# Two transformer layers on one core: one program block for both layers, the second layer's first tile prepared during the first layer, and new written orders

## The chip, the cores and the metric

The kernel runs on one core of a Trainium2 chip. The metric is the device time of one execution in microseconds (us). A core has five engines with instruction streams of their own: TensorE (PE in the profile, with its weight loads as PEld), VectorE (DVE), ScalarE (ACT), GpSimd (POOL) and SyncE (SP), which only starts DMA transfers here. They wait for each other through semaphores. Each stream is executed in the order in which it is written: an instruction that waits holds up all that stands behind it on its engine.

## The reference, cut to what matters

All numbers are float32. The input x has 4 sequences (b) of 1024 rows of 128 values.

```python
# layer 0
xn = layernorm(x)
qkv = einsum('bse,ehd->bshd', xn, qkv_w) + qkv_b          # 16 heads of 64
probs = softmax(where(causal, q @ k.T / 8, -big))          # per sequence and head, 1024 x 1024
x = x + (probs @ v) @ out_w + out_b + ffn(xn)
# layer 1
xn = layernorm(x)
h = layernorm(xn) * ln_w + ln_b
q, k, v, beta = split(h @ w_slow)                          # 16 heads of 64
# for each s and head, over the 4 sequences b = 0..3 as steps of a recurrence:
#   W += sigmoid(beta) * (v - W @ k) outer k ;  out = W @ q     (q, k: elu + 1, normed to sum 1)
x = x + xn + out @ w_out + moe(xn)                         # 8 experts of 256, best 2 by gate
```

## The kernel before, in words

**Layer 0** first works out the feed-forward part for the four sequences, then the attention in 32 units: a unit is one sequence and one pair of heads. The function `unit(u)` of each engine writes out that engine's share of a unit, and a loop calls it for u = 0 to 32 (the last call only finishes what unit 31 left). A unit handles the 8 row tiles of 128 queries in 5 steps (`STEP_ROWS`): 7; 6 and 0; 5 and 1; 4 and 2; 3. For each step:

- PE writes the scores of both heads into the PSUM tiles `pair0` and `pair1` (`score`, L747). A score matmul contracts over 64 rows, so it uses a 64-row part of the array (64*128 in the profile).
- DVE adds the causal mask (`cover`, L473) and takes the negated maxima of the rows (`maximum`, L482).
- ACT writes the exponentials to SBUF (`softmax`, L369); DVE inverts the sums (`invert`, L500); POOL scales (`scale`, L309).
- PE transposes the probabilities (`flip`, L764, full array) into one of two PSUM tiles, and ACT or DVE copies them to `slots` (`keep_flip`).
- One unit later PE multiplies them by the values (`weigh_high`, L783, for the key tiles lo to hi; `weigh_first`, L807 and L811, for the first four query tiles). These matmuls write 64 columns of the array (128*64 in the profile), one head in either half.
- The output projection (`join`, L829) goes through the PSUM tile `misc`, as do the projections of the next unit (`project`, L712, and `project_values`, L725); DVE adds it into x1 (`add_part`, L517).

Both heads share `pair0` and `pair1` from step to step, so the scores of a step wait until the exponentials of the step before have left their bank.

**Layer 1** is a block of its own, started when all engines have left the first. It works through 8 tiles of 128 positions, each with all 4 sequences. The function `tile(t)` of each engine is called for t = -1 to 8 and writes one fixed pattern, in which parts of tiles t-1, t and t+1 stand mixed. For one tile: DVE takes the statistics (L1453, L1457), POOL turns them into scale and shift (`deviation`, L1142 to L1149), ACT norms (`norm`, `second_norm`), PE transposes, and projects to q, k, v (`project`, L1731) and to the experts (`hidden` L1746, `expert` L1760). POOL multiplies keys and queries of the sequences (`key_products` L1173, `query_products` L1183), DVE sums them per head (`sum_keys` L1562, `sum_queries` L1570) and solves the recurrence in small steps (`mixing`). The values are weighted per sequence r ("row r") by r+1 terms: on DVE (`row`, L1618) for rows 0 and 1 and the first two terms of row 3, on POOL for row 2 (`row2`, L1200) and the other two terms of row 3 (`row3_high`, L1212; `HIGH = 2`). The terms of rows 1 and 2 are added up on POOL (`sums`, L1225) before PE transposes them (`flip_row`, L1790); those of row 3 are transposed one by one and added in PSUM. Last, PE projects out (`join`, L1807), DVE adds (`finish`, L1630; `gather`, L1553 for the experts) and SP writes the tile out.

The tables `PLACES`, `given_at` and `made_at` say which of five PSUM tiles each result uses and in which order; `Tally` objects turn written orders into semaphore counts.

## Time and profile before

| | |
|---|---|
| time, median of 3 runs | 1790.3 us (1790.0 to 1790.69) |
| profiled execution, its own time | 1789.99 us |
| its span, from the first to the last instruction | 1788.3 us |
| PE busy | 1725.7 us (97%) |
| DVE busy | 1309.1 us (73%) |
| ACT busy | 1012.0 us (57%) |
| POOL busy | 838.2 us (47%) |

The span leaves out what lies around the instructions (1.69 us here). PE counts as busy while a matmul is in its pipeline; two matmuls overlap, so rows of PE last longer than the distance from the start of one to the start of the next.

### The profile page before, as it was taken

What the parts mean: (1) busy time and instruction counts of PE and PEld (TensorE: products, weight loads), DVE (VectorE), ACT (ScalarE), POOL (GpSimd) and SP (SyncE); (2) the same over time, 40 slices, a digit from 0 to 9 for tenths busy, and PEclk for the clock granted to TensorE, in tenths of its full rate; (3) what the DMA queues carried; (4) which work ended last, traced back from release to release, by engine and by line L of the source; (5) the groups of instructions that cost most, each with busy time, mean ns of one, the idle gap of its engine ahead of it and who ended that gap; (6) DMA issues with size and microseconds to landing.
All of it is one profiled execution on the core that took longest, in us unless ns stands there. A gap on an engine that the chain in (4) does not pass through costs nothing. (4 is left out here: it accounts for less than half of the span.)

```text
span 1788.3 us, 29509 instructions
## 1 busy us (share of the span) xinstructions
PE 1725.7 (97%) x10026; PEld 1046.3 (59%) x10026; DVE 1309.1 (73%) x2730; ACT 1012.0 (57%) x2043; POOL 838.2 (47%) x681
## 2 busy tenths in 40 slices
PE   7989999999999999999999999987899999999995
PEld 4545555555555555555555555554567767767765
DVE  5466766666676676667666666743999999999994
ACT  2255656665665666566566656645565566565551
POOL 2133332333333233233333323322798798798785
PEclk9999999999999999999999999998999999999997
DMA  8000000000000000000000000001000000000000
GB/s 168 0 1 2 1 1 1 1 1 1 1 1 1 1 1 1 1 1 1 1 1 1 1 1 1 1 1 48 0 1 7 7 1 7 7 1 7 7 0 13
DMA packets 30022, 13.59 MB, mean 8 GB/s; under 512 B 17050, under 2 KB 29364, under 8 KB 29876
## 3 DMA queue, kind: packets, MB, share of 16 engines
q1 hardware_dynamic: 29876, 11.70, 2.9%
q8 instruction: 84, 1.38, 0.3%
q14 instruction: 62, 0.51, 0.1%
HBM read 9.60 MB, written 2.10 MB: 7 GB/s over the span
## 5 line engine op out<-in xcount | busy, mean ns | idle before, releaser
L309 POOL TENSOR_SCALAR probs<-probs,recip 128x128 f32<-128x128 f32 (+5 forms) x448 | 331.0, 753 | 760.9 <-DVE recip L500 760.9
L369 ACT ACTIVATE probs<-pair,neg_max 128x1024 f32<-128x1024 f32 (+6 forms) x448 | 331.6, 749 | 202.1 <-DVE neg_max L482 193.4
L482 DVE TENSOR_REDUCE neg_max<-pair 128x1 f32<-128x256 f32 (+7 forms) x512 | 374.1, 752 | 28.9 <-PE pair L747 12.0
L342 ACT ACTIVATE slots<-flip 128x512 f32<-128x512 f32 x384 | 217.8, 595 | 171.1 <-PE flip L764 98.4
L764 PEld LDWEIGHTS flip<-ident,probs 128*128 128x128 f32 x2048 | 226.2, 141 | 139.8 <-POOL probs L309 83.7
L747 PE MATMUL pair<-qk_sb 64*128 64x512 f32 (+3 forms) x1536 | 291.5, 505 | 2.9 <-ACT probs L369 2.9
L764 PE MATMUL flip<-ident,probs 128*128 128x128 f32 x2048 | 284.3, 277 | 3.5 <-ACT slots L342 2.2
L473 DVE TENSOR_TENSOR pair<-pair,mask 128x128 f32<-128x128 f32 x512 | 135.2, 293 | 192.4 <-PE pair L747 192.2
L783 PE MATMUL accum<-slots,v_sb 128*64 128x512 f32 (+3 forms) x1024 | 233.9, 537 | 1.2 <-ACT slots L342 1.2
L747 PEld LDWEIGHTS pair<-qk_sb 64*128 64x128 f32 x1536 | 125.1, 186 | 110.1 <-issue 71.9
L1183 POOL TENSOR_TENSOR prod<-ks,qs 128x1024 f32<-128x1024 f32 (+3 forms) x32 | 180.2, 5630 | 5.6 <-DVE qs L1522 5.0
L1731 PE MATMUL pair<-slow_sb,h_T 128*128 128x512 f32 x384 | 179.6, 597 | 0.5 <-DVE qs L1522 0.5
L712 PE MATMUL misc<-xnT,w_qk 128*128 128x512 f32 x256 | 137.3, 618 | 3.2 <-DVE v_sb L491 1.7
L783 PEld LDWEIGHTS accum<-slots,v_sb 128*64 128x64 f32 x1024 | 51.2, 135 | 123.6 <-issue 123.5
L1731 PEld LDWEIGHTS pair<-slow_sb,h_T 128*128 128x128 f32 x384 | 70.0, 192 | 78.6 <-issue 69.5
L1173 POOL TENSOR_TENSOR prod<-ks 128x1024 f32<-128x1024 f32 (+2 forms) x24 | 109.2, 4549 | 0.0
L500 DVE RECIPROCAL recip<-row_sum 128x2 f32<-128x2 f32 x256 | 37.6, 158 | 81.4 <-ACT probs L369 81.4
L456 DVE COPY slots<-flip 128x512 f32<-128x512 f32 x128 | 87.5, 686 | 11.5 <-PE flip L764 7.1
L1570 DVE TENSOR_REDUCE misc<-prod 128x16 f32<-128x1024 f32 (+3 forms) x32 | 90.3, 2822 | 5.3 <-POOL prod L1183 5.2
L1371 ACT ACTIVATE e_buf<-pair 128x1024 f32<-128x1024 f32 x64 | 65.4, 1021 | 50.2 <-PE pair L1731 50.2
L369 ACT ACTIVATION_READ_ACCUMULATOR probs<-pair,neg_max 128x1 f32 x448 | 91.2, 204 | 0.0
L1746 PE MATMUL flip<-nrm_T,w_sb 128*128 128x512 f32 x176 | 87.5, 601 | 2.3 <-DVE x L1553 1.2
(167 smaller groups left out, 2619.0 us busy)
## 6 DMA issues: line engine op xcount, KB each, us to landing
x<-in_L_attn_x SPq DMA_DIRECT2D x4, 512.0 KB, 5.1
out<-x SPq DMA_DIRECT2D x8, 256.0 KB, 2.3
slow_sb<-in_L_attn_w_slow SPq DMA_DIRECT2D x3, 512.0 KB, 7.9
w_qk<-in_L_attn_qkv_w SPq DMA_DIRECT2D x2, 512.0 KB, 7.1
w_sb<-in_L_ffn_W SPq DMA_DIRECT2D x1, 1024.0 KB
w_v<-in_L_attn_qkv_w SPq DMA_DIRECT2D x1, 512.0 KB, 7.4
bv_bc<-in_L_attn_qkv_b SPq DMA_DIRECT2D x1, 512.0 KB, 7.5
outw_sb<-in_L_attn_out_w SPq DMA_DIRECT2D x1, 512.0 KB, 7.0
```

The costliest lines, as they stand in the source:

```text
L309: pool.tensor_scalar(part, part, recip[:, u % 2, row, h:h + 1], 0.0, ALU.mult, ALU.add).then_inc(scaled, 1)
L342: act.activation(slot_rows(step, h, f), flips[bank][:].rearrange("p (k q) -> p k q", q=P), ACT.Copy).then_inc(flip_kept[bank], 1)
L369: act.activation(dst, pair[h][:, lo:hi], ACT.Exp, bias=neg_max[:, u % 2, row, h:h + 1], accum_out=row_sum[:, u % 2, row, h:h + 1]).then_in ...
L473: dve.tensor_tensor(pair[h][:, hi - P:hi], pair[h][:, hi - P:hi], mask[:], ALU.add).then_inc(covered, 1)
L482: dve.tensor_reduce(out=neg_max[:, u % 2, row, h:h + 1], in_=pair[h][:, lo:hi], axis=AX.X, op=ALU.max, negate=True).then_inc(max_ready, 1)
L712: pe.matmul(misc[:], lhsT=w_qk[:, c, P * n:P * (n + 1)], rhs=xnT[:, u // PAIRS, 512 * half:512 * (half + 1)], start=True, stop=True).then_ ...
L747: last = pe.matmul(pair[h][:, a:z], lhsT=q[part, P * r:P * (r + 1)], rhs=k[part, a - lo:z - lo], start=True, stop=True)
L764: last = pe.transpose(flips[bank][:, P * k:P * (k + 1)], src[:, P * k:P * (k + 1)], ident[:])
L783: last = pe.matmul(accum[D * h:D * (h + 1), at:512], lhsT=values_of(u, k, h), rhs=slots[:, base + at:base + 512], start=k == 0, stop=k == ...
L1173: pool.tensor_tensor(prod[s % 2][:, 0:s, :], ks[:, 0:s, :], ks[:, s:s + 1, :].broadcast_to([P, s, HD]), ALU.mult).then_inc(prod_ready, 1)
L1183: pool.tensor_tensor(prod[s % 2][:, s:2 * s + 1, :], ks[:, 0:s + 1, :], qs[:, s % 2:s % 2 + 1, :].broadcast_to([P, s + 1, HD]), ALU.mult). ...
L1731: last = pe.matmul(places[k][:, 512 * half:512 * (half + 1)], lhsT=h_T[:, P * s:P * (s + 1)], rhs=slow_sb[:, c, 512 * half:512 * (half + 1 ...
```

## The change

The changed kernel computes the same. Five things differ.

1. **Units of layer 0**: the order in `unit(u)` of PE, DVE, ACT and POOL is another, and some `keep_flip` and `keep_att` calls have moved between ACT and DVE. On PE the 8 key tiles of `weigh_high` stood in 8 pieces and stand in two.
2. **Layer 0 prepares layer 1**: the statistics of x1 are taken right after the last addition of each sequence (`second_statistics` in units 8, 16, 24 and at the end; `second_deviation` on POOL); the first tile is normed for the sequences 0 to 2 in unit 28 (`first_norms`, six ACT instructions), and transposed and kept in the places of unit 32's projections (`flip_first`, `keep_first`). Constants are made in layer 0 as well.
3. **One block** holds both layers. The expert weights are loaded into buffers of layer 0 (`xn`, `w_qk`) as soon as those are free; `ks` and `vs` use `xnT` and `qk_sb`.
4. **Layer 1** has no `tile(t)` any more: all 8 tiles are written out one after the other, each engine in its own order, with new places. Tiles 4 to 7 of the sequence come first (`at_of`), since their additions in layer 0 end first.
5. **Row 3**: `HIGH` is 1 (DVE makes one term, POOL three) and POOL adds up row 3 too (`sums(t, 3)`), so `flip_row` transposes 1 term and not 4. Only in the last tile does DVE make all four terms of row 3, and PE transposes every term of rows 1 to 3.

```diff
+                if u > PAIRS and u % PAIRS == 1 and u < UNITS:
+                    second_deviation(u // PAIRS - 1)
...
+            def first_norms():
+                n = at_of(0)
+                act.wait_ge(second_rstd, B - 1)
+                for k, dst in enumerate((nrm, hat)):
+                    for s in range(B - 1):
+                        last = act.activation(dst[:, s, :], x1[:, s, n, :], ACT.Identity, bias=shift1[:, k, s, n:n + 1],
+                                              scale=rstd1[:, k, s, n:n + 1])
+                    last.then_inc(first_normed, 1)
...
+            def second_statistics(u, g):
+                b = u // PAIRS
+                dve.wait_ge(misc_kept, misc_at(u, "o", g))
+                for r in range(GB * g, GB * (g + 1)):
+                    last = dve.bn_stats(stats[:, r, :], x1[:, b, r, :])
+                counted[0] += 1
+                last.then_inc(stats_step, 1)
+                dve.wait_ge(stats_step, counted[0])
+                for r in range(GB * g, GB * (g + 1)):
+                    last = dve.bn_aggr(var1[:, b, r, :], stats[:, r, :])
+                last.then_inc(second_var, 1)
...
                 def add_part(u, g):
...
+                if u % PAIRS == PAIRS - 1:
+                    second_statistics(u, g)
...
-                    weigh_high(u - 1, 0, 1)
+                weigh_high(u - 1, 0, 2)
...
-                    weigh_high(u - 1, 1, 2)
...
+                weigh_high(u - 1, 2, 8)
...
-HIGH = 2
-SUMMED = (1, 2)
+HIGH = 1
...
                 def sums(t, r):
...
+                if r == 3:
+                    pool.wait_ge(high_ready, t + 1)
...
                 def flip_row(t, r, j):
...
-                    many = 1 if r in SUMMED else r + 1
+                summed = r and t < ROWS - 1
+                pe.wait_ge(sum_ready[r] if summed else terms_ready[r], t + 1)
+                many = 1 if summed else r + 1
...
-                for t in range(-1, ROWS + 1):
-                    tile(t)
+            project(0, 0, 0)
+            project(0, 0, 1)
+            flip_nrm(0)
+            flip_hat(0)
+            make_small(0)
+            hidden(0, 1, 1)
```

On PE, in a unit of layer 0 (units 2 to 30 are alike), before: from the scores of step 0 (`pair<-qk_sb 128x512 x4`) on. `accum<-slots` is a piece of `weigh_high`, `flip<-ident,probs` are transposes, `misc<-` are projections.

```order
L747 MATMUL pair<-qk_sb 128x512 x4
L783 MATMUL accum<-slots,v_sb 64x512 x2
L764 MATMUL flip<-ident,probs 128x128 x8
L783 MATMUL accum<-slots,v_sb 64x512 x2
L712 MATMUL misc<-xnT,w_qk 128x512
L783 MATMUL accum<-slots,v_sb 64x512 x2
L747 MATMUL pair<-qk_sb 128x384 x2
L747 MATMUL pair<-qk_sb 128x128 x2
L747 MATMUL pair<-qk_sb 128x512 x2
L783 MATMUL accum<-slots,v_sb 64x512 x2
L764 MATMUL flip<-ident,probs_last 128x128 x4
L764 MATMUL flip<-ident,probs 128x128 x4
```

The same place of PE after the change, from the scores of step 0 to the end of `weigh_high`:

```order
L870 MATMUL pair<-qk_sb 128x512 x4
L906 MATMUL accum<-slots,v_sb 64x512 x4
L887 MATMUL flip<-ident,probs 128x128 x8
L835 MATMUL misc<-xnT,w_qk 128x512
L887 MATMUL flip<-ident,probs_last 128x128 x4
L870 MATMUL pair<-qk_sb 128x384 x2
L870 MATMUL pair<-qk_sb 128x128 x2
L870 MATMUL pair<-qk_sb 128x512 x2
L906 MATMUL accum<-slots,v_sb 64x512 x6
L906 MATMUL accum<-slots,v_sb 64x384 x2
L906 MATMUL accum<-slots,v_sb 64x256 x2
L906 MATMUL accum<-slots,v_sb 64x128 x2
```

The pieces of `weigh_high` have moved together, and the transposes and projections that stood between them stand before or behind.

On POOL, in one tile of layer 1, before: `terms<-vs,M 128x3072` is row 2, `terms<-terms` are the sums, `terms<-vs,M 128x2048` is the high part of row 3.

```order
L1225 TENSOR_TENSOR terms<-terms 128x1024
L1200 TENSOR_TENSOR terms<-vs,M 128x3072
L1225 TENSOR_TENSOR terms<-terms 128x1024 x2
L1142 TENSOR_TENSOR rstd_l<-mv_l,eps 128x4
L1143 TENSOR_SCALAR rstd_l<-mv_l 128x4
L1144 TENSOR_SCALAR neg_mean<-mv_l 128x4
L1147 TENSOR_TENSOR rstd_l<-rstd_l,minus_half 128x8
L1149 TENSOR_TENSOR shift<-rstd_l,neg_mean 128x8
L1183 TENSOR_TENSOR prod<-ks,qs 128x1024
L1212 TENSOR_TENSOR terms<-vs,M 128x2048
L1173 TENSOR_TENSOR prod<-ks 128x1024
```

On POOL after the change, in a late tile (`xnT` is `ks`, `qk_sb` is `vs`):

```order
L1479 TENSOR_TENSOR terms<-terms 128x1024
L1456 TENSOR_TENSOR terms<-qk_sb,M 128x3072
L1419 TENSOR_TENSOR x<-nrm,x 128x4x128
L1479 TENSOR_TENSOR terms<-terms 128x1024 x2
L1466 TENSOR_TENSOR terms<-qk_sb,M 128x3072
L1441 TENSOR_TENSOR prod<-xnT,qs 128x1024
L1433 TENSOR_TENSOR prod<-xnT 128x1024
L1479 TENSOR_TENSOR terms<-terms 128x1024 x3
L1441 TENSOR_TENSOR prod<-xnT,qs 128x2048
```

The five small instructions of `deviation` are gone from the tile, the high part of row 3 has three terms (3072) and not two (2048), and three more sums follow it.

On PE, where layer 0 ends and layer 1 begins, before: `misc<-outw_sb` is the last output projection of layer 0.

```order
L829 MATMUL misc<-outw_sb,att_T 128x128 x8
L238 UNCONDITIONAL_BRANCH
L1677 UNCONDITIONAL_BRANCH
L1702 MATMUL accum<-ident,hat 128x128 x4
L1690 MATMUL flip<-ident,nrm 128x128 x4
L1715 MATMUL flip<-wg_sb,nrm_T 128x8
```

The same place after the change:

```order
L952 MATMUL misc<-outw_sb,att_T 128x128 x8
L2540 UNCONDITIONAL_BRANCH
L2592 MATMUL pair<-slow_sb,h_T 128x512 x4
L2554 MATMUL flip<-ident,nrm 128x128
L2564 MATMUL accum<-ident,hat 128x128
L2575 MATMUL flip<-wg_sb,nrm_T 128x8
```

Two projections of the first tile stand first, and only one transpose of either kind (the fourth sequence) is left to do there.

## Rows read from the trace of the kernel before

**Rows 1.** The page, part 1: busy us, share of the span, instructions.

```profile
PE 1725.7 (97%) x10026; PEld 1046.3 (59%) x10026; DVE 1309.1 (73%) x2730; ACT 1012.0 (57%) x2043; POOL 838.2 (47%) x681
```

**Rows 2.** Stretches: length, busy PE, PEld, DVE, ACT, POOL; clock, DMA share, GB/s.

```profile
85.95:1157.70 1071.75, 1065.74 (x6519) 597.20 (x6518) 729.88 (x1605) 644.80 (x1479) 359.54 (x492) 1.00 0.00 1
1205.50:1299.40 93.90, 74.14 (x300) 45.38 (x300) 63.94 (x143) 50.74 (x80) 46.96 (x24) 0.89 0.08 23
1299.40:1754.00 454.60, 450.19 (x2488) 316.35 (x2488) 437.57 (x788) 268.46 (x401) 383.28 (x120) 1.00 0.02 5
1754.00:1788.30 34.30, 18.78 (x124) 17.87 (x124) 9.94 (x11) 4.07 (x7) 15.90 (x5) 0.69 0.03 9
```

**Rows 3.** Timeline of PE over one unit: start, length, what, how many records.

```profile
605.94 1.08 PE L783 MATMUL accum<-slots,v_sb 128*64 128x512 f32 x4
...
607.98 1.08 PE L783 MATMUL accum<-slots,v_sb 128*64 128x512 f32 x4
608.99 1.12 PE L712 MATMUL misc<-xnT,w_qk 128*128 128x512 f32 x2
610.04 1.08 PE L783 MATMUL accum<-slots,v_sb 128*64 128x512 f32 x4
...
629.94 1.02 PE L712 MATMUL misc<-xnT,w_qk 128*128 128x512 f32 x2
630.80 1.04 PE L764 MATMUL flip<-ident,probs 128*128 128x128 f32 x8
631.74 1.16 PE L829 MATMUL misc<-outw_sb,att_T 128*128 128x128 f32 x8
...
666.41 1.16 PE L829 MATMUL misc<-outw_sb,att_T 128*128 128x128 f32 x8
```

**Rows 4.** Timeline of PE in unit 31, which has no projections.

```profile
1160.95 1.08 PE L783 MATMUL accum<-slots,v_sb 128*64 128x512 f32 x4
...
1162.98 1.94 PE L783 MATMUL accum<-slots,v_sb 128*64 128x512 f32 x8
1164.85 2.00 PE L747 MATMUL pair<-qk_sb 64*128 64x384 f32 x12
```

**Rows 5.** Timelines of DVE and ACT behind the scores of step 0.

```profile
606.06 2.36 DVE L482 TENSOR_REDUCE neg_max<-pair 128x1 f32<-128x1024 f32 x2 [0.36 <-PE pair L747]
...
608.45 1.11 ACT L369 ACTIVATE probs<-pair,neg_max 128x1024 f32<-128x1024 f32 x1
```

**Rows 6.** Groups of layer 1: count, busy us, mean ns, idle before.

```profile
L1225 POOL TENSOR_TENSOR terms<-terms 128x1024 f32<-128x1024 f32 x24 | 56.7, 2362 | 50.5 <-DVE terms L1618 49.2
...
L1212 POOL TENSOR_TENSOR terms<-vs,M 128x2048 f32<-128x2048 f32 x8 | 29.0, 3624 | 1.2 <-PE flip L1790 1.2
...
L1618 DVE TENSOR_TENSOR terms<-vs,misc 128x2048 f32<-128x2048 f32 x16 | 36.5, 2283 | 3.2 <-PE flip L1790 3.1
...
L1453 DVE BATCH_NORM_STATS2 stats<-x 128x6 f32<-128x128 f32 x32 | 6.9, 278 | 0.8 <-POOL score L1132 0.8
...
L1338 ACT ACTIVATE hat<-x,shift,rstd_l 128x128 f32<-128x128 f32 x32 | 13.1, 486 | 12.4 <-POOL shift L1149 12.4
```

**Rows 7.** Timeline of POOL: the same sum in two tiles that follow each other.

```profile
1362.98 2.37 POOL L1225 TENSOR_TENSOR terms<-terms 128x1024 f32<-128x1024 f32 x1 [6.75 <-DVE terms L1618]
...
1429.09 2.37 POOL L1225 TENSOR_TENSOR terms<-terms 128x1024 f32<-128x1024 f32 x1 [6.74 <-DVE terms L1618]
```

**Rows 8.** Timeline of PE between the layers.

```profile
1202.40 1.16 PE L829 MATMUL misc<-outw_sb,att_T 128*128 128x128 f32 x8
...
1214.22 1.09 PE L1702 MATMUL accum<-ident,hat 128*128 128x128 f32 x4 [8.72 <-ACT hat L1338]
```

**Rows 9.** Timeline of the end: POOL's last product, PE's last transposes, DVE's last addition.

```profile
1743.32 8.88 POOL L1183 TENSOR_TENSOR prod<-ks,qs 128x4096 f32<-128x4096 f32 x1
...
1770.76 3.65 PE L1790 MATMUL flip<-ident,terms 128*128 128x128 f32 x16 [1.64 <-POOL terms L1212]
...
1784.84 0.69 DVE L1630 TENSOR_TENSOR x<-flip,x 128x512 f32<-128x512 f32 x1 [21.36 <-PE flip L1807]
```

More of the change, by code:

```diff
@@ L98, in banks_of, with __init__ @@
     return [k for k in range(2) if lo < 512 * (k + 1) and hi > 512 * k]
+GROUPS = (1, 0)
+EARLY = (('qk', 0, 1), ('qk', 1, 0))
 class Tally:
-    def __init__(self, order, units=UNITS):
+    def __init__(self, order, last=()):
         self.order, self.at, n = order, {}, 0
-        for body in range(-1, units + 1):
+        for body in range(-1, UNITS + 1):
             for key, ahead in order:
-                if 0 <= body + ahead < units:
+                if 0 <= body + ahead < UNITS or (body + ahead == UNITS and key in last):
                     n += 1
@@ L155, in layer0 @@
             (('qk', 0, 0), 1), (('o', 1), -1), (('o', 0), -1),
-    ])
+    ], last=EARLY)
     weighed_at = Tally([
@@ new lines, in values_of, with join @@
+            def values_of(u, k, h):
+                at = 2 * D * (u % 2) + D * h
+                return v_sb[:, u // 2 % 2, k, at:at + D]
+            def join(u, g):
+                if done(u):
+                    return
+                use = misc_at(u, "o", g)
+                misc_at.meet(u, "o", g)
+                if use > 1:
+                    pe.wait_ge(misc_kept, use - 1)
+                pe.wait_ge(att_kept, accum_at(u, g))
+                for r in range(GB):
+                    at = P * ROW_ORDER[g].index(r)
+                    last = pe.matmul(misc[:, P * r:P * (r + 1)], lhsT=att_T[:, g, at:at + P], rhs=outw_sb[:, u % PAIRS, :],
+                                     start=True, stop=True)
+                last.then_inc(misc_made, 1)
@@ L1721, in project @@
-                def project(t, s, c):
-                    if done(t):
-                        return
-                    k, use = given(t, "project", s, c)
-                    given_at[k].meet(t, "project", s, c)
-                    if use > 1:
-                        pe.wait_ge(place_kept[k], use - 1)
-                    n, each = given(t, "hat")
-                    pe.wait_ge(place_kept[n], each)
-                    for half in range(2):
-                        last = pe.matmul(places[k][:, 512 * half:512 * (half + 1)], lhsT=h_T[:, P * s:P * (s + 1)],
-                                         rhs=slow_sb[:, c, 512 * half:512 * (half + 1)], start=True, stop=True)
-                    last.then_inc(place_made[k], 1)
@@ L1864, in _ @@
-                for t in range(-1, ROWS + 1):
-                    tile(t)
+                for n, each in latest(given, t, [("score",)] + [("row", r, j) for j in range(2)]):
+                    pe.wait_ge(place_kept[n], each)
+                dst = places[k][:, P * r:P * (r + 1)]
+                pe.matmul(dst, lhsT=score_T[:, P * r:P * (r + 1)], rhs=b2_sb[:], start=True, stop=False)
+                for n in range(PAIRS):
+                    last = pe.matmul(dst, lhsT=outs_T[:, r, n, :], rhs=wout_sb[:, n, :], start=False, stop=n == PAIRS - 1)
@@ new lines, in join @@
+                last.then_inc(joined, 1)
+            project(0, 0, 0)
+            project(0, 0, 1)
+            flip_nrm(0)
+            flip_hat(0)
+            make_small(0)
+            hidden(0, 1, 1)
+            project(0, 1, 1)
+            hidden(0, 1, 0)
+            hidden(0, 0, 0)
+            project(0, 1, 0)
+            hidden(0, 0, 1)
+            hidden(0, 2, 0)
+            expert(0, 0)
+            project(0, 2, 1)
+            expert(0, 1)
+            hidden(0, 2, 1)
+            project(0, 2, 0)
```

3898 lines of the change are left out of this document (2508 added, 1390 removed), and 22 rows, old and new, of tables (exps_at, prods_at, sums_at).

## The prediction

> **What bounds the kernel now.** I read the page first: PE is busy 97% of the span, the next engine 73% [rows 1]. Such shares are means over unlike stages, so I read the busy times by stretch. The reader is to see three stages. In the units of layer 0 PE is busy for practically the whole stretch (1065.74 of 1071.75 us) at the full clock, and DVE, ACT and POOL have room (730, 645, 360 us). In the steady tiles of layer 1 three engines are nearly full: PE 450.19, DVE 437.57 and POOL 383.28 of 454.6 us. Before and behind them PE is idle for 19.8 of 93.9 and 15.5 of 34.3 us, with the granted clock down to 0.89 and 0.69 on average [rows 2].
>
> Then the timeline of PE. The output projection of one unit starts at 631.74, that of the next at 666.41: a unit takes 34.67 us [rows 3]. The same sum of two tiles of layer 1 starts at 1362.98 and at 1429.09: a tile takes 66.11 us [rows 7]. Between the last projections of layer 0 (from 1202.40) and the end lie 585.9 us [rows 8].
>
> **The units: fewer changes of the array's shape.** The unit has the same matmuls after the change. What can differ is what stands beside what. Scores use 64 rows of the array, `weigh` 64 columns, all else the whole. Four records of `weigh_high` take 1.01 us from start to start (607.98 to 608.99) [rows 3], eight in one run 1.87 (1162.98 to 1164.85) [rows 4]: 0.86 for four, and 0.15 on top for each run. A projection between two such runs takes 1.05 (608.99 to 610.04), among whole-array matmuls 0.86 (629.94 to 630.80), 0.19 less. Eight transposes between two runs take 1.03 (605.94 to 607.98, less 1.01), among whole-array matmuls 0.94 (630.80 to 631.74) [rows 3]. So a guest between two `weigh` runs costs 0.15 + 0.19 or 0.15 + 0.09 us for two changes of shape: 0.12 to 0.17 each.
>
> In the written orders of PE I count the changes of shape in a unit: 23 before, 13 after (the pieces of `weigh_high` have moved together). Ten fewer give 1.2 to 1.7 us; I take 1.5, in the middle. Units 1 to 30 are full ones, in which PE never waits: 30 x 1.5 = **45 us**. Units 0, 31 and the clearing up, where PE waits for others anyway, I count at nothing.
>
> The Trainium skill, "TensorEngine Tiling (Array Packing)", Key Properties, says that changing the tiling mode drains TensorE, and "TensorE: Matmul & The Clock Gate", Single matmul latency, puts such a drain at about 166 ns warm. By these 10 x 0.166 x 30 = 50 us would be gained and not 45, and the time would be 1700; the rows lie at or below that figure.
>
> This is worth something only if nobody makes PE wait at 33.2 us a unit. I walked the new order once with the durations of the rows. After the scores of step 0 (they end at 605.94) DVE's maxima run to 608.42 and ACT's last exponential to 609.56, so the next scores may start 3.6 us later [rows 3, 5]. In the new order 1.87 + 0.94 + 0.86 + 0.47 + 0.15 = 4.3 us of matmuls stand between: 0.7 us to spare. At the other steps I find 0.2 to 1.2 us; least before `project(u + 1, 1, 1)`, since DVE has to reach `keep_values(u + 1, 1)`, which it meets between two maxima, and before both output projections. A walk misses small things, so I add 0.1 us a unit: **+3 us**.
>
> **What is put into the units.** `second_statistics` puts 4 instructions of 278 ns [rows 6] and 4 smaller ones, about 1.3 us, behind each of two additions on DVE in units 8, 16 and 24. Queued behind them are the last mask and maxima of the unit; ACT's last exponentials wait for these, and the next unit's scores for those. Some 1.5 of the 2.6 us find room; I take 1.1 us of stall, three times: **+3.3 us**. `first_norms` are six ACT instructions of 486 ns [rows 6], 2.9 us ahead of the copy that `weigh_high` needs and of the first exponentials of unit 28; 1.1 us of it is idle time: **+1.8 us**. POOL's `second_deviation` and the constants fall into POOL's idle time, two thirds of the stretch [rows 2]; without that cover they would be 3 us three times.
>
> **Layer 1.** I sum it by DVE, which is nearest to full if PE gets shorter. DVE's work now is 63.94 + 437.57 + 9.94 = 511.5 us [rows 2]. Away go the statistics (6.9 us [rows 6] and the aggregates, some 3) and in seven tiles half of a 2.28 us product of row 3 [rows 6], 8.0 us; the last tile has four terms and not two, +2.3, and the first tile's two copies come to DVE, +0.5. That leaves 496.4 us. In the steady stretch DVE was idle for 17.0 us in 6.88 tiles (454.6 / 66.11), 2.5 a tile [rows 2, 7]: 20 us in eight. DVE's stream starts 7.5 us after the first of the last two output projections (one addition, statistics, POOL's deviation, a norm of one column block; before, the first transpose came 11.8 us after it, at 1214.22 [rows 8], and DVE's stream later still), and I allow 3 us of holes behind it, before there is work from the experts. At the end, after DVE's last product: 32 transposes, 6.5 us if the clock is halved again as for the 16 of 3.65 us [rows 9], a copy, the output projection and the addition, 3.3, and 2.8 from there (1785.53) to the end of the span; 1.8 of it are in the 496.4 already: 10.8 us. Sum: 7.5 + 3 + 496.4 + 20 + 10.8 = 537.7 us, say 538, against 585.9: **-48 us**.
>
> Does it hold for the other two? PE loses 24 transposes a tile, of 0.94 / 8 us [rows 3] at most: 66.1 - 2.8 = 63.3. POOL is busy 55.7 us a tile (383.28 / 6.88) [rows 2, 7]; it gets three sums of 2.36, 7.1, and a third term, half of 3.62, 1.8, and loses `deviation`, some 2.5 [rows 6]: 62.1 us. My DVE sum is 64.5 a tile with its idle time. So all three stay just below it. The sums on POOL are paid from its idle time of 10.4 us a tile; 6.75 of that is one wait for DVE [rows 7]. If that wait stays where it is, the cover is gone and a tile takes up to 62.1 + 10.4 = 72.5.
>
> **Sum.** 1789.99 (the profiled execution's own time: 1788.3 and 1.69 around it) - 45 + 3 + 3.3 + 1.8 - 48 = 1705.1. The median of the runs is 0.3 above this execution: **1705 us**.
>
> **The rivals.**
> - *PE waits in the units* (chance 0.2). The pairs' banks go round scores, maxima, exponentials, scores, and my margins are as small as 0.2 us. For it: DVE and ACT instructions have strict places, so one late copy delays the next scores. Against it: before, PE had no wait at all at 34.67. If the new unit takes 34.1, 0.9 more than I say, this is 30 x 0.9 = 27 us: 1732.
> - *Layer 1 gets stuck between three full engines* (0.2). POOL at 62.1 and PE at 63.3 leave no room, and a sum that waits for DVE's row holds up the products that DVE waits for. With tiles of 67 us, 2.5 above mine, 8 x 2.5 = 20 us: 1725.
> - *The grouping gives nothing* (0.07): the 0.15 us belongs to something else than the shape. Then units keep 34.67 and the time is 1705 + 45 = 1750.
> - *Slower* (0.03). POOL's `sums(t, 3)` wait for the whole of row 3; behind them stand the products of the next tile, for which DVE waits, and DVE makes the row after that late: if each tile went round this ring, with nothing beside it, the gain of 85 us would be used up from 64.5 + 85 / 8 = 75.1 us a tile; at 78 us it is 1705 + 8 x 13.5 = 1813. The wait of 6.75 us that exists speaks for it, the written order, in which other products stand between, against.
>
> **How the numbers follow.** The forecast has 0.5, with 1690 to 1718 as its own range: 1.7 and not 1.5 us a unit is -6, DVE's idle time at 1 us a tile -12, a change of shape at 0.12 us +9. The first two rivals reach to about 1735. 1685 to 1735 leaves out the fourth part of the first rival, the last two rivals (0.10) and a little below: 0.2. A difference of 0.2% (3.6 us) is about what can be told from no change here. All cases but the last lie far under the time before: faster 0.96, same 0.01, slower 0.03.
>
> **What would show it.** The start of one unit's output projection to the next: 33.0 to 33.4 us, with no gaps on PE; about 35 in units 8, 16, 24 and 28. A run of 24 records of `weigh_high` without pause. The second layer's steady tiles 64 to 65 us, DVE at 96% or more, POOL above 95%. Between the layers no PE gap over 3 us, and no halved clock there. I am wrong if PE shows gaps that end with ACT's exponentials (first rival), if POOL's sums wait (second), or if the records around a joined run cost as much as before (third).

## The result, and the profile after

The changed kernel takes **1690.7 us** (median of 4 runs, 1689.2 to 1692.2) against 1790.2 before in the same session: a ratio of 0.9445, 95% interval 0.9428 to 0.9461. The forecast was 1705 us, with 1685 to 1735 as its range.

Part 1 of the page, and the chain of the work that ended last, after:

```profile
PE 1655.9 (98%) x9882; PEld 1041.9 (62%) x9882; DVE 1329.2 (79%) x2765; ACT 999.9 (59%) x2009; POOL 885.8 (52%) x683
...
PE 96%; DVE 2%; ACT 1%; issue 1%; DMA 0%; POOL 0%; DVEq 0%; ACTq 0%
```

PE has lost 69.8 us of busy time and still fills 98% of the span [rows 1]. Only 144 of its records are gone, so most of that time is not work that left but work that takes less.

The stretches that answer to [rows 2]: the units up to the last but one first output projection, and three pieces of the second layer.

```profile
85.36:1143.91 1058.55, 1047.05 (x6689) 630.54 (x6689) 780.13 (x1730) 648.74 (x1488) 381.25 (x521) 1.00 0.01 2
1168.00:1230.00 62.00, 60.39 (x260) 35.76 (x259) 55.84 (x105) 42.95 (x65) 47.70 (x19) 0.97 0.00 1
1230.00:1660.00 430.00, 429.66 (x2287) 294.28 (x2286) 418.93 (x746) 271.58 (x404) 420.73 (x109) 1.00 0.02 5
1660.00:1690.40 30.40, 25.28 (x217) 24.05 (x216) 20.93 (x30) 7.95 (x14) 11.22 (x2) 0.98 0.06 19
```

The third row is the one to look at. In 430 us of steady tiles PE is busy 99.9%, DVE 97.4% and POOL 97.8% of the time; before, it was 99%, 96% and 84%. The two stretches beside it have filled up as well, and their mean granted clock is 0.97 and 0.98, no longer 0.89 and 0.69. The clock still falls to 0.50, the lower of its two levels, once between the layers. The first row below is of the changed kernel, the other two of the kernel before, whose second layer has 0.50 in two far longer stretches:

```profile
1174.00:1177.00 3.00, 3.00 (x6) 1.45 (x6) 2.53 (x10) 1.43 (x6) 2.35 (x1) 0.50 0.00 0
```

```profile
1209.00:1225.00 16.00, 8.63 (x28) 6.23 (x29) 0.80 (x7) 6.51 (x17) 3.76 (x6) 0.50 0.39 118
1752.00:1775.00 23.00, 8.97 (x40) 8.26 (x41) 11.24 (x11) 3.44 (x6) 16.10 (x6) 0.50 0.04 11
```

PE over one unit, the same place as in [rows 3]:

```profile
612.37 1.16 PE L952 MATMUL misc<-outw_sb,att_T 128*128 128x128 f32 x8
...
624.89 2.00 PE L870 MATMUL pair<-qk_sb 64*128 64x384 f32 x12
626.82 4.09 PE L906 MATMUL accum<-slots,v_sb 128*64 128x512 f32 x24
630.84 1.09 PE L887 MATMUL flip<-ident,probs 128*128 128x128 f32 x8
...
645.42 0.82 PE L952 MATMUL misc<-outw_sb,att_T 128*128 128x128 f32 x5
```

The 24 records of `weigh_high` stand in one run. From one output projection to the next it is 33.05 us (34.67 before): 1.61 us a unit. Six key tiles in one run take 4.02 us from start to start.

Where the extra work stands, PE does wait. The scores of unit 9's first step, behind the statistics of the sequence that has just ended, and the first `weigh_high` of unit 28, behind `first_norms`:

```profile
387.90 1.13 PE L870 MATMUL pair<-qk_sb 64*128 64x512 f32 x4 [1.15 <-ACT probs_last L437]
```

```profile
1022.78 1.94 PE L906 MATMUL accum<-slots,v_sb 128*64 128x512 f32 x8 [1.77 <-ACT slots L399]
```

The distances with the statistics are 34.49, 34.50 and 34.50 us, that with the norms 35.23; three others are 33.4, all the rest 33.06 up to unit 30.

Between the layers (before: [rows 8]) and at the end ([rows 9]) on PE:

```profile
1163.40 1.16 PE L952 MATMUL misc<-outw_sb,att_T 128*128 128x128 f32 x8
1165.34 1.16 PE L952 MATMUL misc<-outw_sb,att_T 128*128 128x128 f32 x8 [0.78 <-DVE x L620]
1166.33 3.60 PE L2592 MATMUL pair<-slow_sb,h_T 128*128 128x512 f32 x8
1170.88 0.33 PE L2554 MATMUL flip<-ident,nrm 128*128 128x128 f32 x1 [0.95 <-ACT nrm L1650]
...
1680.22 3.66 PE L2642 MATMUL flip<-ident,terms 128*128 128x128 f32 x32
1684.66 0.46 PE L2655 MATMUL accum<-b_sb,score_T 128*128 128x128 f32 x2 [0.78 <-ACT outs_T L1624]
```

The first work of the second layer starts 2.93 us behind the first of the last two output projections, where it was 11.8, and no gap of PE between the layers reaches 1 us.

**Where the 97.9 us of the span are.** The first of the last two output projections starts 39.0 us earlier (1163.40 against 1202.40); from there to the end it is 527.0 us and not 585.9: 58.9 us less. The additions that end a tile (`finish`) cut these 58.9 in three. Up to the first of them the second layer takes 124.5 us (before 157.6), -33.1; the six tiles behind it 62.6 us each (before 65.3 on average), -15.7; the rest 26.6 us (36.7), -10.1.

### The profile page after: what moved, and what is told of

It is laid out like the page before. It is cut to its first block, busy times and chain, and to the rows that moved or that the text cites. A ratio compares the mean times of both kernels' runs of the same rounds, so it can differ in the third digit from the quotient of the medians.

```text
span 1690.4 us, 29061 instructions
## 1 busy us (share of the span) xinstructions
PE 1655.9 (98%) x9882; PEld 1041.9 (62%) x9882; DVE 1329.2 (79%) x2765; ACT 999.9 (59%) x2009; POOL 885.8 (52%) x683
## 4 chain that ended last, share of the span: by engine, by line
PE 96%; DVE 2%; ACT 1%; issue 1%; DMA 0%; POOL 0%; DVEq 0%; ACTq 0%
PE pair L870 16%; PE flip L887 16%; PE accum L906 11%; PE pair L2592 10%; PE misc L835 7%; PE flip L2617 5%; PE flip L2605 4%; PE misc L952 4%; PE misc L848 3%; PE flip L2657 3%; PE accum L930 3%; PE pair L801 3%; PE accum L2605 2%; PE accum L2617 2%; PE accum L934 2%; PE flip L811 1%
## 5 line engine op out<-in xcount | busy, mean ns | idle before, releaser
L363 POOL TENSOR_SCALAR probs<-probs,recip 128x256 f32<-128x256 f32 (+5 forms) x448 | 331.3, 754 | 707.8 <-DVE recip L589 707.7
L437 ACT ACTIVATE probs<-pair,neg_max 128x768 f32<-128x768 f32 (+5 forms) x448 | 331.9, 749 | 210.3 <-DVE neg_max L571 210.3
L571 DVE TENSOR_REDUCE neg_max<-pair 128x1 f32<-128x768 f32 (+7 forms) x512 | 372.7, 754 | 33.2 <-PE pair L870 10.3
L906 PE MATMUL accum<-slots,v_sb 128*64 128x512 f32 (+3 forms) x1024 | 192.9, 519 | 3.5 <-ACT slots L399 3.5
L1441 POOL TENSOR_TENSOR prod<-xnT,qs 128x1024 f32<-128x1024 f32 (+3 forms) x32 | 180.2, 5634 | 6.5 <-DVE xnT L2134 4.8
L534 DVE COPY slots<-flip 128x512 f32<-128x512 f32 x192 | 131.8, 687 | 24.2 <-PE flip L887 20.4
L1433 POOL TENSOR_TENSOR prod<-xnT 128x1024 f32<-128x1024 f32 (+2 forms) x24 | 109.1, 4548 | 10.4 <-DVE xnT L2134 10.4
L1479 POOL TENSOR_TENSOR terms<-terms 128x1024 f32<-128x1024 f32 x42 | 99.2, 2362 | 5.7 <-DVE terms L2220 3.4
L2617 PEld LDWEIGHTS flip<-w_qk,hid 128*128 128x128 f32 x720 | 86.2, 192 | 17.7 <-issue 13.3
L1633 ACT ACTIVATE hid<-flip,columns 128x512 f32<-128x512 f32 x86 | 58.6, 683 | 52.5 <-PE flip L2605 47.5
```

The costliest lines, as they stand in the source:

```text
L363: pool.tensor_scalar(part, part, recip[:, u % 2, row, h:h + 1], 0.0, ALU.mult, ALU.add).then_inc(scaled, 1)
L437: act.activation(dst, pair[h][:, lo:hi], ACT.Exp, bias=neg_max[:, u % 2, row, h:h + 1], accum_out=row_sum[:, u % 2, row, h:h + 1]).then_in ...
L571: dve.tensor_reduce(out=neg_max[:, u % 2, row, h:h + 1], in_=pair[h][:, lo:hi], axis=AX.X, op=ALU.max, negate=True).then_inc(max_ready, 1)
L906: last = pe.matmul(accum[D * h:D * (h + 1), at:512], lhsT=values_of(u, k, h), rhs=slots[:, base + at:base + 512], start=k == 0, stop=k == ...
L1441: pool.tensor_tensor(prod[s % 2][:, s:2 * s + 1, :], ks[:, 0:s + 1, :], qs[:, s % 2:s % 2 + 1, :].broadcast_to([P, s + 1, HD]), ALU.mult). ...
L2617: last = pe.matmul(places[k][:, P * s:P * (s + 1)], lhsT=hid[:, e % 2, j, P * s:P * (s + 1)], rhs=w2_sb[:, e, j, :], start=j == 0, stop=j ...
```

## The experiments

**1. The grouping taken back, in the changed kernel.** Only PE's order of the unit is touched:

```diff
-                weigh_high(u - 1, 0, 2)
+                weigh_high(u - 1, 0, 1)
                 flip(u - 1, 3, 0, 1, 0)
                 flip(u - 1, 3, 1, 1, 1)
+                weigh_high(u - 1, 1, 2)
                 project(u + 1, 1, 0)
+                weigh_high(u - 1, 2, 3)
                 flip(u - 1, 4, 1, 0, 0)
                 score(u, 1, 1)
                 score(u, 1, 0)
-                weigh_high(u - 1, 2, 8)
+                weigh_high(u - 1, 3, 6)
                 flip(u, 0, 0, 1, 1)
+                weigh_high(u - 1, 6, 7)
                 flip(u, 0, 1, 1, 0)
                 project_values(u + 1, 0)
+                weigh_high(u - 1, 7, 8)
```

> The changed kernel with the two runs of weigh_high cut into six pieces again on TensorE (key tiles 0, 1, 2, 3 to 5, 6, 7), with transposes and projections between them: 20 changes of the array's shape in a unit and not 13. Theory (the changes of shape cost 0.12 to 0.17 us each): 7 x 0.16 = 1.1 us a unit, the distance from unit to unit goes from 33.06 to 34.2 us, and the time from 1690.7 to about 1725 us. Rival (the gain of the units is from the other orders, not from the grouping): 33.1 us a unit, about 1691 us. Above 1730 would mean waits of PE.

Measured: 1725.6 us (ratio to before 0.9637, 0.9623 to 0.9652), 34.9 us above the changed kernel. PE's timeline, the output projection of two units that follow each other:

```profile
595.29 1.16 PE L952 MATMUL misc<-outw_sb,att_T 128*128 128x128 f32 x8
...
601.68 1.08 PE L906 MATMUL accum<-slots,v_sb 128*64 128x512 f32 x4
602.69 1.09 PE L887 MATMUL flip<-ident,probs 128*128 128x128 f32 x8
603.71 1.08 PE L906 MATMUL accum<-slots,v_sb 128*64 128x512 f32 x4
...
629.44 1.16 PE L952 MATMUL misc<-outw_sb,att_T 128*128 128x128 f32 x8
```

34.15 us, 1.10 us more for seven changes of shape more, with no wait: 0.156 us each. The same matmuls in another neighbourhood cost that much. The change as a whole gives 1.61 us for ten: 0.161. Counted in the traces, what differs are the changes between 128*64 (64 columns) and the full array: 13 in a unit before, 10 here, 3 in the changed kernel. All other changes of shape together, those from and to the scores' 64*128, are 10 in each of the three. So 0.16 us is what this one kind costs; the price of the others does not follow from these runs.

**2. The grouping alone, in the kernel before.**

```diff
-                    weigh_high(u - 1, 0, 1)
+                    weigh_high(u - 1, 0, 2)
                     flip(u - 1, 3, 0, 1, 0)
                     flip(u - 1, 3, 1, 1, 1)
-                    weigh_high(u - 1, 1, 2)
                     project(u + 1, 1, 0)
-                    weigh_high(u - 1, 2, 3)
+                    flip(u - 1, 4, 0, 0, 0)
                     score(u, 1, 1)
                     score(u, 1, 0)
-                    weigh_high(u - 1, 3, 4)
-                    flip(u - 1, 4, 0, 0, 0)
+                    weigh_high(u - 1, 2, 8)
                     flip(u, 0, 1, 0, 1)
-                    weigh_high(u - 1, 4, 5)
                     project_values(u + 1, 0)
-                    weigh_high(u - 1, 5, 6)
                     flip(u, 0, 1, 1, 0)
                     flip(u - 1, 4, 1, 0, 1)
-                    weigh_high(u - 1, 6, 7)
                     score(u, 2, 1)
                     score(u, 2, 0)
-                    weigh_high(u - 1, 7, 8)
```

> The kernel before with weigh_high in two runs on TensorE (key tiles 0 and 1; 2 to 7) and nothing else changed: 14 changes of shape in a unit and not 23. Theory (shape alone): 9 x 0.16 = 1.4 us a unit, 33.2 us from unit to unit, -43 us, about 1747 us. Rival (the new orders of VectorE and ScalarE are needed for it): PE waits behind copies and exponentials that stand where they stood; 34 to 35 us a unit, 1770 to 1795 us. If the grouping gives nothing: 1790 us without PE waits.

Measured: 1792.7 us, ratio 1.0012 (1.0003 to 1.0021): nothing is gained. A unit takes 34.64 us. But PE's work did get shorter: in the stretch up to the last but one first output projection (1096.90 us before, 1098.48 here) it is busy 1053.37 us and not 1089.64.

```profile
85.95:1184.43 1098.48, 1053.37 (x6678) 626.76 (x6677) 739.01 (x1645) 658.58 (x1514) 369.61 (x506) 1.00 0.00 1
```

```profile
85.95:1182.85 1096.90, 1089.64 (x6680) 610.25 (x6680) 746.26 (x1645) 660.09 (x1514) 369.66 (x506) 1.00 0.00 1
```

The first row is of this kernel, the second of the kernel before over the same stretch. The 36 us that PE saves have turned into idle time. In one unit PE waits 0.52 and 0.63 us, 1.15 together; without them a unit would take 33.49 us, 1.18 less than before, or 0.13 for each of nine changes. Why it is less than the 0.16 of experiment 1 is not shown. The timeline of PE, then that of ACT, show one of the places:

```profile
477.53 0.66 PE L764 MATMUL flip<-ident,probs 128*128 128x128 f32 x4
...
480.56 1.99 PE L747 MATMUL pair<-qk_sb 64*128 64x256 f32 x12 [0.63 <-ACT probs L369]
```

```profile
478.22 0.60 ACT L342 ACTIVATE slots<-flip 128x512 f32<-128x512 f32 x1 [2.37 <-PE flip L764]
478.72 0.36 ACT L369 ACTIVATE probs<-pair,neg_max 128x128 f32<-128x128 f32 x1
...
479.40 1.01 ACT L369 ACTIVATE probs<-pair,neg_max 128x896 f32<-128x896 f32 x1
```

The transpose `flip(u, 0, 1, 0, 1)` now stands behind the long run, at 477.53. ACT's copy of it stands in ACT's order ahead of three exponentials whose maxima were ready, so ACT idles 2.37 us, the exponentials come late, and the next scores wait 0.63 us for them. The grouping moves guests of the run to later places, and the other engines' orders have to follow.

**3. The new orders of the units alone, in the kernel before.** All `unit(u)` functions of PE, DVE, ACT and POOL, the tables that count them and the choice of PSUM tile for each transpose (`FLIP_BANK`) are those of the change; blocks, statistics, norms and the second layer are as before.

> The kernel before with the changed written orders of the units on all engines (and the tables that count them), and nothing else: two blocks, no early statistics or norms, the second layer as before. Theory (the grouping on PE pays when the other engines' orders let it, and owes nothing to the rest of the change): 33.06 us from unit to unit, 30 x 1.6 = -48 us, less what units 0 and 31 lose, about 1745 us. Rival (the units need something of the common block, or the second layer gives time back): 1755 us or more.

Measured: 1743.7 us, ratio 0.9737 (0.9722 to 0.9751), -46.6 us; 33.05 us a unit, and the first of the last two output projections stands at 1155.77 and not at 1202.40. The gain of the units is there to the full without any other part of the change, 7.6 us more than in the changed kernel, 6.5 of it in the four units in which the changed kernel has the extra work. Experiments 1 to 3 together: the fewer changes of shape are the gain, and the orders written anew with them (those of the other engines, and the rest of PE's own) are its condition. Which of the new orders are needed was not tried apart.

**4. Row 3 alone, in the kernel before.** One term on DVE and three on POOL, and POOL adds up row 3.

```diff
-HIGH = 2
-SUMMED = (1, 2)
+HIGH = 1
+SUMMED = (1, 2, 3)
...
                     pool.wait_ge(terms_ready[r], t + 1)
+                    if r == 3:
+                        pool.wait_ge(high_ready, t + 1)
...
                     key_products(t, 1)
+                    sums(t - 1, 3)
                     query_products(t, 1)
```

> The kernel before with only row 3 changed: one term on VectorE, three on GpSimd, and GpSimd adds the four up, so that PE transposes one. Theory A (the moved load alone makes the gain of the second layer): PE 2.7 us a tile less, GpSimd 55.7 + 8.9 = 64.6 us a tile at most, tiles of about 64.6 us and not 66.1, 1776 to 1780 us. Theory B (the fixed pattern of a tile can't take it; the written order is needed): GpSimd keeps part of its 10.4 us of waits a tile, tiles of 67 to 72 us, 1795 to 1835 us.

Measured: 1834.8 us, ratio 1.0247 (1.0232 to 1.0262): 44 us slower. POOL's timeline, the first sum of two tiles that follow each other, as in [rows 7]:

```profile
1440.41 2.37 POOL L1227 TENSOR_TENSOR terms<-terms 128x1024 f32<-128x1024 f32 x1 [6.76 <-DVE terms L1621]
...
1496.27 8.91 POOL L1183 TENSOR_TENSOR prod<-ks,qs 128x4096 f32<-128x4096 f32 x1
1511.94 2.37 POOL L1227 TENSOR_TENSOR terms<-terms 128x1024 f32<-128x1024 f32 x1 [6.76 <-DVE terms L1621]
```

A tile takes 71.53 us. POOL works through 64.8 of them and then waits 6.76 us for DVE's row 1, the wait of before. DVE's timeline has the other half:

```profile
1438.06 2.28 DVE L1621 TENSOR_TENSOR terms<-vs,misc 128x2048 f32<-128x2048 f32 x1
...
1477.36 2.29 DVE L1573 TENSOR_REDUCE misc<-prod 128x32 f32<-128x2048 f32 x1 [5.59 <-POOL prod L1183]
...
1509.59 2.28 DVE L1621 TENSOR_TENSOR terms<-vs,misc 128x2048 f32<-128x2048 f32 x1
```

POOL's product for query row 1 comes only behind the three new sums; DVE waits 5.59 us for it at 1477.36, is late with row 1 at 1509.59 by that, and POOL's sum of row 1 waits for this row. From POOL's sum to DVE's sum it is 36.9 us (1440.41 to 1477.36), from there to POOL's next sum 34.6: this ring of two halves is the tile. What is put into POOL's half makes it longer, while POOL stands idle in DVE's. The granted clock is 0.50 for some 7 us in each of these tiles, but that is not what makes them long: POOL works without a wait through its half (1440.41 to 1477.33) and the one wait of DVE in its half is 0.33 us, for POOL and not for PE.

**5. Row 3 not summed, in the changed kernel.** `sums(t, 3)` is left out for tiles 0 to 6, and `flip_row` transposes its four terms one by one.

```diff
-            sums(0, 3)
...
-                summed = r and t < ROWS - 1
+                summed = r and t < ROWS - 1 and r != 3
                 pe.wait_ge(sum_ready[r] if summed else terms_ready[r], t + 1)
+                if r == 3 and t < ROWS - 1:
+                    pe.wait_ge(high_ready, t + 1)
```

> The changed kernel without the sums of row 3 on GpSimd: PE transposes all four terms of row 3 in tiles 0 to 6, 24 transposes more a tile; GpSimd has 3 sums of 2.36 us less a tile. If PE is the bound of the second layer (what the trace after suggests): 24 x 0.114 = 2.7 us a tile, 19 us in seven, about 1710 us. If VectorE is (my sum before the result): about 1691 us. If GpSimd is: up to 7 x 7 = 50 us less, down to 1645 us.

Measured: 1707.8 us, ratio 0.9539 (0.9523 to 0.9555): +17.1 us for 168 transposes. A steady stretch of it:

```profile
1228.01:1658.01 430.00, 429.66 (x2338) 299.03 (x2337) 405.21 (x727) 268.08 (x397) 362.04 (x86) 1.00 0.02 5
```

PE is full; POOL, with 84%, and DVE, with 94%, have room that buys nothing. So in the written order the move of row 3's sums to POOL is worth 17 us; in the fixed pattern the sums and the third term on POOL together cost 44 (experiment 4).

**6. and 7. A little more work for DVE, and for POOL, in the changed kernel.** Each tile makes one sum over 128x1024 twice (DVE), or adds 128x256 constants twice (POOL); the extra results go to a spare buffer.

```diff
+                if r == 0:
+                    if t:
+                        dve.wait_ge(spare_step, t)
+                    dve.tensor_reduce(out=spare_out[:, 0:H], in_=prod[0][:, 0, :].rearrange("p (h d) -> p h d", h=H),
+                                      axis=AX.X, op=ALU.add).then_inc(spare_step, 1)
```

```diff
+                pool.wait_ge(late_loaded, 16 * 6)
+                for k in range(2):
+                    if t or k:
+                        pool.wait_ge(spare_step, 2 * t + k)
+                    pool.tensor_tensor(spare_out[:].rearrange("p (s e) -> p s e", s=2), wout_sb[:, 0:2, :], wout_sb[:, 2:4, :],
+                                       ALU.add).then_inc(spare_step, 1)
```

> The changed kernel with one more sum over 128x1024 on VectorE in each tile of the second layer (the sum for query row 0 made a second time into a spare buffer), some 1.1 us. If VectorE sets the tiles (my sum): 8 x 1.1 = +9 us, 1700 us. If PE does, with VectorE's 11 us of idle time in 430 as room: +0 to +3 us, 1691 to 1694 us.

> The changed kernel with two more additions of 128x256 on GpSimd in each tile of the second layer (into a spare buffer), some 1.3 us a tile, ahead of the residual. If GpSimd sets the tiles: 8 x 1.3 = +10 us, 1701 us. If PE does and GpSimd has room: +0 to +3 us, 1691 to 1694 us.

The groups of the added instructions (busy us, mean ns), DVE's kernel and POOL's kernel:

```profile
L2178 DVE TENSOR_REDUCE spare_out<-prod 128x16 f32<-128x1024 f32 x8 | 9.7, 1208 | 0.0
```

```profile
L1424 POOL TENSOR_TENSOR spare_out<-wout_sb 128x256 f32<-128x256 f32 x16 | 11.8, 740 | 0.6
```

Measured: 1700.2 us with 9.7 us more on DVE (+9.5), and 1695.4 with 11.8 more on POOL (+4.7). By the medians DVE's time is paid in full, though PE's row of the changed kernel seemed to say that PE alone was the bound. The medians overstate both a little, since the executions of one kernel differ in their mean granted clock, and their times with it. Compared between executions with the same mean clock (0.997), DVE's kernel takes 1700.2 us against 1692.2, +8.0, and POOL's 1695.5, +3.3. PE shows it: in the steady stretch of DVE's kernel its busy time is 424.69 of 430 us, with waits such as

```profile
1261.26 0.66 PE L2648 MATMUL accum<-ident,terms 128*128 128x128 f32 x4 [0.98 <-DVE x L2162]
```

My expectation that DVE's 11 us of idle time would take the work was wrong: in the same stretch of DVE's kernel DVE still idles 11.1 of 430 us. My reading is that this idle time lies in other places than the added work; no run has tried that. Of POOL's addition some 60% to 70% found room. Which of two nearly full engines sets the pace can't be told from the busy times of the page; here both do.

**8. Two blocks again, in the changed kernel.** All engines meet between the layers, and the expert weights are loaded after that.

```diff
             layer1(block, sem, sbuf, kept, early, shared, ended, W1, W2, b2_sb, b2, late, out)
...
+        with nc.Block() as block:
```

> The changed kernel with the second layer in a block of its own again (all engines meet between the layers, and the expert weights start to load only then); first tile, orders and row 3 as changed. Theory (the common block is worth something at the boundary): the last additions, the meeting and the loads of 2 MB stand ahead of the first expert matmuls; +5 to +12 us, 1696 to 1703 us. Rival (the early preparation does it all, and the block is nothing): within 2 us of 1690.7.

Measured: 1697.0 us, ratio 0.9478 (0.9465 to 0.9491), +6.3 us. PE between the layers:

```profile
1165.05 1.16 PE L953 MATMUL misc<-outw_sb,att_T 128*128 128x128 f32 x8 [0.79 <-DVE x L621]
1168.95 5.37 PE L2593 MATMUL pair<-slow_sb,h_T 128*128 128x512 f32 x8 [2.74 <-PEq L78]
```

The first projection starts 5.84 us behind the first of the last two output projections and not 2.93, with a wait of 2.74 us for the meeting. The next eight matmuls then take 5.37 us where they took 3.60: the granted clock is 0.50 from 1170.1 to 1173.4, and again from 1177 to 1183, and its mean in the 62 us from there on is 0.92 (0.97 in the changed kernel). So what the second block costs is the meeting and, behind it, a longer time at the lower clock. I had also expected the loads to stand in the way, but PE's waits up to 1250 us hold none for the expert weights. Between the two profiled executions the part behind the output projection is 5.6 us longer, 532.6 us and not 527.0.

**9. No early first tile, in the changed kernel.** `first_norms` and `flip_first` are left out (`EARLY = ()`); tile 0 is normed, transposed and kept for all four sequences after the last addition. The start of the second layer is written in another order for it: ACT's norms ahead of its first exponentials, PE's transposes ahead of its first projections.

> The changed kernel without the early norms and transposes of the first tile: all four sequences of tile 0 are normed, transposed and kept after the last addition of the first layer (statistics of sequences 0 to 2 still early). Theory (the early tile is worth several us at the boundary): 2.2 us come back in unit 28; behind the last addition stand eight norms of 0.49 us and not two, eight transposes and not two, and full copies ahead of the first projection: +5 to +9 us there, 1694 to 1698 us. Rival (hidden by what else starts there, all the gain of the boundary is the block and the order): 1688 to 1691 us.

Measured: 1696.9 us, ratio 0.9472 (0.9456 to 0.9488), +6.2 us. PE between the layers:

```profile
1162.10 1.16 PE L950 MATMUL misc<-outw_sb,att_T 128*128 128x128 f32 x8
...
1170.11 1.09 PE L2562 MATMUL accum<-ident,hat 128*128 128x128 f32 x4 [4.91 <-ACT hat L1658]
1171.56 1.11 PE L2552 MATMUL flip<-ident,nrm 128*128 128x128 f32 x4 [0.36 <-ACT nrm L1648]
1172.46 5.50 PE L2587 MATMUL pair<-slow_sb,h_T 128*128 128x512 f32 x8
```

The first projection stands 10.4 us behind the first of the last output projections and not 2.9. In this execution 1.6 us more are lost in unit 31, to a lower clock (below), and 1.8 are won in unit 28. From the first of the last output projections to the end it takes 533.4 us, 6.4 more than in the changed kernel, with the granted clock at 0.50 for twice as long. Less the 1.8 of unit 28, the early tile is worth some 4.6 us in this execution, and 6.2 by the medians.

**10. The extra work moved, in the changed kernel.** The statistics go into units 9, 17 and 25, cut in four pieces where DVE idles 0.9 to 1.1 us; `second_deviation` a unit later; `first_norms` behind ACT's first exponentials of unit 28, where ACT otherwise idles 3.3 us.

```diff
-                if u == UNITS - 4:
-                    first_norms()
...
                 keep_flip(u - 1, 3, 1, 1, 1)
+                if u == UNITS - 4:
+                    first_norms()
...
-                if u % PAIRS == PAIRS - 1:
-                    second_statistics(u, g)
...
                 maximum(u, 6, 1)
+                late = u > PAIRS and u % PAIRS == 1 and u < UNITS
+                if late:
+                    take_stats(u // PAIRS - 1, 1)
                 keep_att(u - 1, 1)
                 invert(u, 0)
+                if late:
+                    take_var(u // PAIRS - 1, 1)
...
                 keep_flip(u, 1, 0, 0, 0)
+                if late:
+                    take_stats(u // PAIRS - 1, 0)
...
                 keep_flip(u, 0, 1, 0, 1)
+                if late:
+                    take_var(u // PAIRS - 1, 0)
```

> The changed kernel with the extra work of the units put where its engine is idle: the statistics of x1 in units 9, 17 and 25, in four idle times of VectorE of 0.9 to 1.1 us, GpSimd's deviation a unit later, and the six norms of unit 28 in ScalarE's idle time of 3.3 us ahead of the exponentials of row 6. Theory (the 1.15 us waits of PE in units 8, 16, 24 and the 1.8 us in unit 28 come from where they stand): those units take 33.1 us and not 34.5 and 35.2; 3 x 1.4 + 2.1 = -6 us, about 1684.5 us. Rival (the work itself makes something late wherever it stands): 1688 to 1692 us.

Measured: 1686.1 us median of 5 runs (1682.6 to 1687.9), ratio to before 0.9410 (0.9398 to 0.9423); the interval lies below that of the changed kernel (0.9428 to 0.9461). The best runs are 1682.6 and 1689.2 us, 6.5 apart. In the trace units 8, 16 and 24 take 33.05 to 33.06 us and unit 28 33.40; the last but one first output projection stands at 1137.48 and not at 1143.91, 6.4 us earlier, as expected. The last one stands only 5.1 us earlier, since unit 31 takes 1.4 us longer at a lower clock (below). DVE's timeline shows a piece of the statistics in its hole, with the copy behind it still waiting for PE:

```profile
396.44 0.86 DVE L604 BATCH_NORM_STATS2 stats<-x 128x6 f32<-128x128 f32 x4
397.52 0.69 DVE L597 COPY att_T<-accum 128x512 f32<-128x512 f32 x1 [0.22 <-PE accum L917]
```

This is the fastest kernel of the study.

## Why the prediction was right, step by step

- **Changes of shape (-45 us).** Right in mechanism and nearly in size: 1.61 us a unit against my 1.5, 0.161 us a change. Experiment 1 shows it from the other side (0.156). The figure of 166 ns that I took from the Trainium skill ("TensorE: Matmul & The Clock Gate", Single matmul latency) is there the fixed part of the latency of one bf16 matmul at the higher clock, which that section links to TensorE's drain. That a change of shape costs as much was an estimate of mine from it. The trace agrees: 0.161 and 0.156 us are 3% and 6% less.
- **Unforeseen waits in the units (+3 us).** Three units of 33.4 us make 1.0; unit 28 is a fourth, since it takes 33.39 without the norms as well (experiment 9). The sum had no term for the start of the units: their first output projection stands at 147.44 us and not at 146.31, 1.1 later. The granted clock there is 0.50 twice in this execution, near 99 and 109 us; whether that is all of the 1.1 is not shown. But experiment 2 shows that my first rival was no idle worry: with only the grouping on PE it comes true in full, PE's idle time rises by 38 us and the gain is gone. It is absent where the other engines' orders changed too (experiment 3); my walk through them had found 0.2 to 1.2 us of room.
- **Statistics (+3.3) and early norms (+1.8).** Measured 3 x 1.43 = 4.3 for the statistics. Unit 28 is 2.2 us longer than most, and 1.8 longer than the same unit without the norms (experiment 9), as forecast. I had let 1.5 of 2.6 us of statistics find room; 1.2 did. Experiment 10 shows that both cost nothing at another place.
- **Units in sum:** -39.0 against -36.9.
- **The second layer (-48 us, measured -58.9): the size was off.** The step that failed is the idle time in my sum by DVE. DVE's busy time from the first of the last output projections on is 499.0 us in the trace (my sum: 496.4). To these I had added 41.3 us of idle time (10.5 + 20 + 10.8); it is 28.0. In the first 12.6 us DVE idles 4.5 (I had 10.5), in the tiles 14.3 (20), in the tail 9.2 (10.8).

```profile
1163.40:1176.00 12.60, 10.21 (x47) 6.37 (x46) 8.10 (x30) 6.70 (x13) 6.35 (x11) 0.92 0.00 0
1176.00:1663.78 487.78, 487.44 (x2554) 330.17 (x2553) 473.48 (x845) 310.21 (x459) 466.95 (x120) 1.00 0.02 4
1663.78:1690.40 26.62, 21.50 (x183) 20.27 (x181) 17.43 (x20) 6.16 (x10) 7.44 (x2) 0.98 0.07 21
```

  I had carried over the idle time of the fixed pattern, and a halved clock for the last 32 transposes: 6.5 us, and they took 3.66. (The 6.5 doesn't even follow from its row: 16 at 3.65 us make 7.3 for 32.) Experiment 6 supports the choice of DVE as the engine to sum by (8.0 to 9.5 of 9.7 us are paid), but PE, at 99.9% of the steady stretch, was just as much a bound: experiment 5 puts 2.4 us a tile back on PE, and they are paid. Two signs that I had named did not come: the tiles take 62.6 us on average and not 64 to 65, and between the layers the clock is at 0.50 from 1174 to 1177 us, where I had said that it would not be.
- **The second rival** (stuck between three full engines, 67 us a tile) did not happen: POOL is at 97.8% and yet PE waits less than 1 us in the steady stretch. **The slower rival** named the ring by which it could happen, POOL's sums, the products behind them and DVE's row; experiment 4 is that ring, with tiles of 71.5 us and the wait of 6.76 us unchanged. The order written out does without it: in the changed kernel the sums' waits for DVE's terms come to 3.4 us over all tiles together.

```profile
L1479 POOL TENSOR_TENSOR terms<-terms 128x1024 f32<-128x1024 f32 x42 | 99.2, 2362 | 5.7 <-DVE terms L2220 3.4
```

  I had put the chance of this ring at 0.03 by the written order alone. Which of its moves breaks the ring was not tried apart.
- **Where the 99.5 us come from.** Orders of the units 46.6 (experiment 3), less 7.6 for extra work and the slower units; one block 6.3 and the early tile 6.2 by the medians (experiments 8 and 9); row 3's sums 17.1 (experiment 5). The rest, some 31 us by difference, is the order of the second layer written out, with the statistics that left it, the one term of row 3 that DVE no longer makes, and the full clock where it was at 0.50 for 16 us at the start and 23 us at the end. These last parts were not tried apart, and such differences need not add up exactly.

## What to carry to other kernels

Where matmuls of unlike array shapes alternate, count the changes of shape: here each between 64 columns and the full array cost 0.16 us. A regrouping on one engine moves the work that stood between, so look at the orders of the engines that feed it and copy for it; alone it was worth nothing here. Before load is moved to an engine with idle time, look whether that idle time is the wait of a ring that the load lengthens: here such a move cost 44 us. Extra work did no harm in holes that the timeline shows, in pieces that fit them, and cost 6 us where the changed kernel has it. And before a small difference between two medians is read, compare the granted clocks of their executions.

## What the runs showed of the hardware

The granted clock of PE fell to 0.50 in the same place of the program in some executions and not in others. In unit 31 PE waits 1.70 to 1.71 us for ACT's copy, in the changed kernel and in experiments 5 to 10 alike, and only in the executions of 9 and 10 is the clock lower behind it. The timelines of the matmuls behind that wait, in the changed kernel and in experiment 10:

```profile
1151.67 1.94 PE L906 MATMUL accum<-slots,v_sb 128*64 128x512 f32 x8 [1.70 <-ACT slots L399]
```

```profile
1145.24 2.84 PE L917 MATMUL accum<-slots,v_sb 128*64 128x512 f32 x8 [1.70 <-ACT slots L399]
```

and the stretch around it in experiment 10, with a mean granted clock of 0.76 (1.00 in the changed kernel):

```profile
1144.00:1151.00 7.00, 5.59 (x22) 2.87 (x24) 1.20 (x4) 1.91 (x5) 2.48 (x4) 0.76 0.00 0
```

It cost 1.4 us there and 1.6 in experiment 9. It is not the only such place. The profiled execution of the changed kernel has 0.50 near 99, 109 and 1174 us, that of experiment 9 not near 99:

```profile
98.90:102.00 3.10, 3.00 (x10) 1.93 (x11) 0.93 (x3) 2.67 (x8) 0.56 (x1) 0.50 0.00 0
```

Such falls go with the spread of the times. The runs of the changed kernel at 1689.2 us have a mean granted clock of 0.999, those at 1692.2 have 0.997; in experiment 10 it is 0.999 at 1682.6 us and 0.996 to 0.997 at 1686 to 1688. An estimate from these means: 0.002 of 1690 us are 3.4 us, and the two groups of the changed kernel lie 3.0 apart. Which of the falls is missing in the faster executions is not known, since one execution of each kernel was profiled.
